# Tile loop of a graph layer: second one-hot half turned at the first tile, register loads behind queued work

## What is computed

```python
def head(w1, bb1, w2, bb2, a1, aab1, a2, aab2):
    feats = jnp.maximum(x @ w1 + bb1, 0.0) @ w2 + bb2
    x_cat = jnp.concatenate([feats[row], feats[col], elem[:, None]], axis=1)
    hid = jnp.maximum(x_cat @ a1 + aab1, 0.0)
    e1 = jax.nn.leaky_relu((hid @ a2 + aab2)[:, 0], negative_slope=0.2)
    w = jnp.exp(e1 - jnp.max(e1))
    pooled = jax.ops.segment_sum(w[:, None] * feats[col], row, num_segments=n)
    row_sum = jax.ops.segment_sum(w, row, num_segments=n) + 1e-10
    return pooled / row_sum[:, None]
...
x = _layernorm(x + gnn(x, edge_index, edge_weight), axis=-1)
```

## Time and profile before

| | |
|---|---|
| median of 3 runs | 5230.21 us (5229.04 to 5233.76) |
| profiled execution | 5190.44 us, span 5188.7 us |
| PE busy | 4402.2 us (85%) |
| DVE busy | 4550.7 us (88%) |
| ACT busy | 3761.1 us (72%) |
| POOL busy | 2702.7 us (52%) |
| mean granted PE clock | 0.956 |
| tile loop, mean DMA rate | about 218 GB/s |

### The profile page before, as it was taken

How to read it: one execution, slowest core, us unless ns; L and a number is a source line. 1 busy time by engine, 2 the same in 40 slices (tenths; PEclk the granted TensorE clock), 3 DMA queues, 4 the chain that set the end, 5 groups by cost and what they waited for, 6 DMA issues and landing times.

```text
span 5188.7 us, 133139 instructions
## 1 busy us (share of the span) xinstructions
PE 4402.2 (85%) x24914; PEld 3093.9 (60%) x24915; DVE 4550.7 (88%) x25629; ACT 3761.1 (72%) x12720; POOL 2702.7 (52%) x2834
## 2 busy tenths in 40 slices
PE   1499899999986899999999999999999999999920
PEld 0255555555554666767677767767677767767610
DVE  7799999999998789888899889889898889898853
ACT  0467766766762688888888888888888888888832
POOL 1266666666666555555555555555555555555522
PEclk9799999999997999999999999999999999999965
DMA  2032333333333777777777777777777777777623
GB/s 79 23 73 67 78 72 71 75 74 72 69 78 93 227 216 218 218 219 217 216 218 217 217 218 219 217 218 216 217 218 216 219 215 219 215 220 216 200 87 117
DMA packets 287022, 850.50 MB, mean 164 GB/s; under 512 B 98946, under 2 KB 138114, under 8 KB 286966
## 3 DMA queue, kind: packets, MB, share of 16 engines
q0 software_dynamic: 169920, 673.54, 46.8%
q1 hardware_dynamic: 74638, 160.14, 9.7%
q10 hardware_dynamic: 42408, 16.21, 1.2%
HBM read 738.46 MB, written 111.26 MB: 164 GB/s over the span
## 4 chain that ended last, share of the span: by engine, by line
PE 29%; ACT 25%; DVE 6%; issue 4%; DMA 4%; DVEq 1%; POOL 0%; ACTq 0%; POOLq 0%; SPq 0%
ACT z L1092 17%; PE psum L949 12%; PE psum L953 7%; PE psum L936 6%; DVE z L1503 3%; ACT onehot L1121 3%; DMA out_dram<-z 3%; ACT onehot_t L1110 3%; PE psum L962 2%; ACT onehot L1125 2%; PE psum L973 1%; DVE z L1493 1%; PE psum L921 1%; DVE acc L1552 1%; DVEq L1552 0%
## 5 line engine op out<-in xcount | busy, mean ns | idle before, releaser
L734 POOL DMA_INDIRECT z<-qf_table,rec x1664 | 1593.6, 958 | 1567.0 <-PE psum L936 1035.8
L1092 ACT ACTIVATE z<-z 128x64 f32<-128x64 f32 x6656 | 1651.5, 336 | 56.6 <-ACT z L1099 56.3
L949 PE MATMUL psum<-p_win,onehot_t 128*128 x9984 | 1434.0, 276 | 207.7 <-ACT onehot_t L1110 90.5
L949 PEld LDWEIGHTS psum<-p_win,onehot_t 128*128 128x128 bf16 x9984 | 963.9, 97 | 777.8 <-issue 460.6
L936 PE MATMUL psum<-z,onehot 128*128 128x260 f32 x3328 | 1027.2, 391 | 2.8 <-DVE acc L1552 1.9
L953 PE MATMUL psum<-z,ident 128*128 128x258 f32 x3328 | 1004.0, 383 | 0.0
L1503 DVE SCALAR_TENSOR_TENSOR z<-z,a_b 128x129 f32<-128x129 f32 x3328 | 893.0, 292 | 0.0
L1503 DVE SCALAR_TENSOR_TENSOR z<-psum,a_b 128x129 f32<-128x129 f32 x3328 | 822.6, 283 | 0.0
L1552 DVE TENSOR_TENSOR acc<-acc,psum 125x260 f32 x1664 | 698.7, 420 | 78.6 <-PE psum L936 48.8
L1493 DVE TENSOR_TENSOR z<-z,psum 128x258 f32<-128x258 f32 x1664 | 691.9, 416 | 39.4 <-PE psum L953 29.6
L666 POOL DMA_INDIRECT sorted_rows<-z x300 | 483.3, 1611 | 406.9 <-DVE z L1384 162.4
(11 more groups left out here) (221 smaller groups left out, 6363.0 us busy)
## 6 DMA issues: line engine op xcount, KB each, us to landing
p_table<-acc SPq DMA_DIRECT2D x100, 377.9 KB
p_win<-p_table SPq DMA_DIRECT2D x100, 377.9 KB
qf_table<-acc SPq DMA_DIRECT2D x75, 378.9 KB
z<-qf_table,rec POOLq DMA_INDIRECT x1664, 4.6
acc<-in_x_dram SPq DMA_DIRECT2D x25, 500.0 KB
z<-in_x_dram SPq DMA_DIRECT2D x20, 625.0 KB
out_dram<-z ACTq DMA_DIRECT2D x20, 625.0 KB
qf_table<-z SPq DMA_DIRECT2D x25, 378.9 KB
```

What stands on the lines that cost most here:

```text
L734: pool.indirect_dma_start(out=z_t[:, o + j, :], out_offset=None, in_=qf_table, in_offset=bass.IndirectOffsetOnAxis(ap=rec[:, o + j, 3:4].b ...
L949: mm = pe.matmul(to, onehot_t[:, j, :], p_flat[:, bass.ds((w % 2) * (3 * ZW) + (part * ZW + o), n)], start=(part == 0), stop=(part == 2 an ...
L1092: op = act.activation(z_t[:, slot, o:o + DO], z_t[:, slot, o:o + DO], ACT.Copy, scale=z_t[:, slot, o + DO:o + HF])
```

## The change

- PE turns half 1 of a step behind tile 0 instead of tile 2.
- ACT copies it between the weights of tiles 5 and 6 of its step before, not at the head of the step.
- PE does the sum of a step's last tile at the head of the step after, behind that step's first register load, and has one more step at its end for it.
- The register loads are taken apart: on PE one at the head of a step and one between the product and the sum of tile 3; on DVE one behind the adds of tile 0 and one behind those of tile 4.
- On DVE, the accumulator's scaling and the adds of the sums come behind the tile's own dot products instead of ahead of them.

```diff
--- before.py
+++ after.py
@@ -464,7 +464,7 @@
             return nc.s_assert_within((pack // (1 << 7 * j)) % 128 if j else pack % 128, 0, W - 1,
                                       skip_runtime_bounds_check_because="the table is clipped at W - 1")
 
-        def pipeline(eng, step):
+        def pipeline(eng, step, extra=0):
 
             step(-1, SPB - 1)
             for k in range(SPB):
@@ -472,7 +472,7 @@
             with nc.Fori(1, BODIES, engines=bass.OrderedEngineSet([eng.engine]), hint_back_edge=True) as i:
                 for k in range(SPB):
                     step(i, k)
-            for n in range(BODIES * SPB, NSB + 2):
+            for n in range(BODIES * SPB, NSB + 2 + extra):
                 step(n // SPB, n % SPB)
 
 
@@ -928,9 +928,13 @@
                 def tile(off, j):
                     return i * RING + (k + off) * SB + j
 
-                def sum_up(j):
-
-                    t, slot = tile(-2, j), ((k - 2) * SB + j) % RING
+                def load_windows(q):
+
+                    packs[q] = pe.value_load(win_pack[0:1, bass.ds((i * SPB + k) * (SB // 4) + q, 1)], min_val=0, max_val=(1 << 28) - 1)
+
+                def sum_up(off, j):
+
+                    t, slot = tile(off, j), ((k + off) * SB + j) % RING
                     pe.wait_ge(s_wf, t + 1)
                     since(pe, s_acc, t - 1)
                     pe.matmul(psum[:, 4 + j % 2, 0:H * HF], onehot[:, slot, :], z_t[:, slot, ZW:QW], start=True, stop=True)\
@@ -973,13 +977,15 @@
                     pe.matmul(psum[:, 7, P:P + H], ones_f[0:H, :], max_diag[:, (k - 1) % SPB, :], start=True, stop=True)\
                       .then_inc(s_max_b, 1)
 
+                packs = [None] * (SB // 4)
                 if live(i, k, 0):
-                    packs = [pe.value_load(win_pack[0:1, bass.ds((i * SPB + k) * (SB // 4) + q, 1)], min_val=0, max_val=(1 << 28) - 1)
-                             for q in range(SB // 4)]
+                    load_windows(0)
+                if live(i, k, -3):
+                    sum_up(-3, SB - 1)
                 for j in range(SB):
                     if live(i, k, 0):
                         hidden_src(j)
-                    if j == SB // 4 and live(i, k, 0):
+                    if j == 0 and live(i, k, 0):
                         turn(0, 1)
                     if j == SB // 4 and live(i, k, -1):
                         max_t()
@@ -987,10 +993,12 @@
                         max_to_all()
                     if j == SB - SB // 4 and live(i, k, 1):
                         turn(1, 0)
-                    if live(i, k, -2):
-                        sum_up(j)
-
-            pipeline(pe, step)
+                    if j % 4 == 3 and j < SB - 1 and live(i, k, 0):
+                        load_windows(j // 4 + 1)
+                    if j < SB - 1 and live(i, k, -2):
+                        sum_up(-2, j)
+
+            pipeline(pe, step, extra=1)
 
 
             pe.wait_ge(s_c_pick, KS)
@@ -1130,8 +1138,6 @@
                     act.dma_start(rec[:, kn * SB:(kn + 1) * SB, :].rearrange("p t n -> p (t n)"),
                                   rec_d[:, bass.ds((i * SPB + (k + 2)) * (SB * 4), SB * 4)]).then_inc(s_rec[kn], 16)
 
-                if live(i, k, 0):
-                    take_turned(0, 1)
                 if live(i, k, 1):
                     onehots(1, 0)
                 if live(i, k, -1):
@@ -1145,6 +1151,8 @@
                         take_turned(1, 0)
                     if j == SB // 2 and live(i, k, 1):
                         onehots(1, 1)
+                    if j == SB - 3 and live(i, k, 1):
+                        take_turned(1, 1)
 
             pipeline(act, step)
 
@@ -1478,9 +1486,11 @@
                 def sbn(off):
                     return i * SPB + (k + off)
 
-                if live(i, k, -2):
-                    packs = [dve.value_load(win_pack[0:1, bass.ds(sbn(-2) * (SB // 4) + q, 1)], min_val=0, max_val=(1 << 28) - 1)
-                             for q in range(SB // 4)]
+                packs = [None] * (SB // 4)
+
+                def load_windows(q):
+                    packs[q] = dve.value_load(win_pack[0:1, bass.ds(sbn(-2) * (SB // 4) + q, 1)], min_val=0, max_val=(1 << 28) - 1)
+
                 kk, kp, o = (k - 1) % SPB, (k - 2) % SPB, (k - 1) % SPB * SB
                 ev, er = e_val[:, o:o + SB, :], e_raw[:, o:o + SB, :]
 
@@ -1560,21 +1570,23 @@
                        .then_inc(s_decayed, 1)
 
                 Q = SB // 4
-                before_row = {0: [(-2, decay_sums)]}
                 chain = {0: [(-1, bias), (-1, leaky), (-1, tiles_max)], Q: [(-1, heads_max), (-1, diagonal)],
                          2 * Q: [(-1, new_shift), (-1, shifted)]}
                 for j in range(SB):
-                    for off, work, *args in before_row.get(j, []):
-                        if live(i, k, off):
-                            work(*args)
                     if live(i, k, 0):
                         add_rows(j)
-                    between = [(-2, add_sums, j)] + chain.get(j, [])
+                    if j % 4 == 0 and live(i, k, -2):
+                        load_windows(j // 4)
+                    between = chain.get(j, [])
                     for n in range(max(H - PEH, len(between))):
+                        if n < H - PEH and live(i, k, 0):
+                            own_dot(j, n)
                         if n < len(between) and live(i, k, between[n][0]):
                             between[n][1](*between[n][2:])
-                        if n < H - PEH and live(i, k, 0):
-                            own_dot(j, n)
+                    if live(i, k, -2):
+                        if j == 0:
+                            decay_sums()
+                        add_sums(j)
 
             pipeline(dve, step)
 
```

## The result

The changed kernel takes 6025.83 us (median of 4 runs, 6019.9 to 6026.52) against 5230.3 us for the kernel before: a ratio of 1.1517, interval 1.1497 to 1.1537. It is 796 us slower, 3.86 us for each of the 206 steps of the ring; the forecast was 750 us and 3.64 us.

What follows compares the result with a forecast made beforehand. A 15.58 us ring of waits between PE and ACT was taken as the bound. The new ring 17.5 + load 0.2 + clock 1.5 = 19.2 us, 3.64 above 15.56; 206 x 3.64 = 750, so 5230 + 750 = 5980 us, range 5600 to 6200.

Steps and rivals of the forecast that it cites:

- the ring: Tile 4's product on PE, ACT's first-half copy and second-half one-hots, PE's turn, back to that product: 17.5 us a step.
- step 2: PE's turn moved behind tile 0 waits for ACT's one-hots and closes a ring of 17.47, say 17.5 us a step.
- step 6: PE's clock falls after 2.6 to 3.0 us idle at the turn: 1.5 us a step, between 0 and 3.4.
- The mean of 2.0 us from the earlier trace: Full-speed work lost on PE after each of twenty idle stretches before the tile loop, in the profile before the change.
- step 3: Register loads: nothing gained on DVE; PE's load between tile 3's product and sum adds 0.2 us a step.
- The bound of 0.66: Upper limit in us for one PE register load, from two loads together; the range was 0 to 0.66.
- steps 4 and 5: Last tile's sum behind the next head on PE, decay and sum behind DVE's dot products: nothing, the latter -0.1 to +0.1.
- own range: Range for the main case, wait and clock fall: 5830 to 6200 us around 5980, chance 0.62.
- The old ring: Tile 4's product, first-half turn, ACT's copies of both halves and work between, back to that product: 15.58 us, the period.
- step 1: ACT's second-half copy ahead of weights six and seven cuts the 15.58 us ring: alone worth up to 1.7 us a step.
- That the clock stays: Rival: PE's turn waits but the idle stretch is too short to lower the clock: 17.7 us a step, 5671 us, chance 0.20.
- The faster side: Rival: ACT's one-hots are ready when PE reaches the turn, so PE's 13.9 us plus 0.4 decide: 4970 us, chance 0.08.

Runs made afterwards that it cites:

- the kernel with the filler: The changed kernel with 20 products of the identity with itself on PE behind tile 0, ahead of the waiting turn: 5595.46 us, ratio 1.0703.
- the first experiment: The changed kernel with only PE's turn of the second half put back behind tile 2: 5048.23 us, ratio 0.9657.
- the third experiment: The kernel before with only the turn behind tile 0 and the copy between weights 5 and 6: 6033.06 us, ratio 1.1546.
- the second experiment: The changed kernel with turn and copy put back, leaving only register loads, late eighth sum and DVE's order changed: 5217.52 us, ratio 0.9981.

## Why the prediction was right

**The ring, step 2.** Its four edges in the changed kernel, from the timeline: H4 3015.69 to copy 3021.08, 5.39 (5.50 forecast); copy to the end of the one-hots, 6.31 (6.32); to the turn at 3027.45, 0.06 (0.05); turn to H4 at full clock, in the kernel with the filler 3000.67 to 3006.32, 5.65 (5.60). The sum is 17.41 against 17.47. The 13 periods of the changed kernel that kept the clock are 17.41 or 17.42 us long, and the filler's mean is 17.46. That the one line decides is shown by the first and the third experiment, that it does so by a ring, and not by a single wait, by the places behind tile 1 and the one-hots behind weight 2.

**The clock, step 6.** The mechanism was right and the size too small: 1.5 us a step forecast, 2.09 measured. Two terms of it failed. The idle stretch was put at 2.6 to 3.0 us and is 3.0 to 3.9 in 194 of 199 steps, because H0 comes earlier than thought: it now starts 1.54 us behind H7 like any tile (3021.24 to 3022.78), where it took 2.40 (3007.13 to 3009.53 in the kernel before), and 0.3 to 0.6 us of that were counted. The load at the head costs PE nothing, L957 to S7 takes 3003.16 to 3003.61. And the mean of 2.0 us from the earlier trace rows was lowered to 1.5 for a shorter stretch and for loss inside the idle time; 2.0 would have been nearly right. The earlier trace rows had nothing, 1.7 or 3.4 us lost, in 4, 8 and 8 of 20; here it is nothing in 13 periods of 199, 1.5 us in the mean in 92 and 2.9 in 94. By the Trainium skill, "TensorE: Matmul & The Clock Gate", section "HAM oscillation — how this bites in real kernels", parted bursts of matmuls pay in every burst; the trace agrees nearly, with a fall in 186 periods of 199.

**The register loads, step 3.** On DVE at nothing: right, 10 us in all in the second experiment. On PE 0.2 us were put on the ring; the changed kernel shows 0 there. The bound of 0.66 was sound all the same: once the one-hots held PE up less, the same load cost up to 0.46 us, 0.21 in the mean. The changed kernel's trace has a load by itself (L933): 0.30 us. The Trainium skill's 0.2 us a register load ("Runtime: NRT & Kernel Launch", section "Instruction fetch mechanics"), by which it vanishes behind H3, is lower than that 0.30; that it vanishes agrees with the changed kernel (0) and not with the first experiment (up to 0.46 behind 1.1 us of queued products).

**The late sum and DVE's order, steps 4 and 5.** At nothing; together with the loads they gained 0.2% in the second experiment, and 0.3% that is not clear of noise by the third. Not foreseen was that ACT's first-half one-hots wait 665.3 / 153 = 4.3 us a step for the sum of tile 3, which stands behind the turn. It costs nothing, as ACT would wait for the exponentials anyway.

**The sum.** 17.47 + 0.2 + 1.5 = 19.2 forecast; 17.41 + 0 + 2.09 = 19.50 measured, the period in the trace. The clock's term was 0.6 us too small, the load's 0.2 too large, and that these erred in opposite ways, which brings the sum within 0.3 us, is luck. The difference was also worked out against 15.56 us from an execution of 5190 us and added to a median from a slower chip: between the two profiled executions it is 829 us, between the medians 796. And the own range of 5830 to 6200 us doesn't follow from its terms: 17.5 with 0 to 0.6 for the load and 0.7 to 2.6 for the clock is 18.2 to 20.7 us a step, 5774 to 6289 us. The old ring (step 1) was drawn as one path, though PE's 189.6 us of waiting were for the copy in 82.8 only and 64.5 for DVE. Breaking it helps all the same: the copy alone takes 2.5% off, 0.64 us a step ((5234.51 - 5103.45) / 206) of the 1.7 that were its upper end. The loads stand in the way of part of the rest.

**The rivals.** That the clock stays needed a filler to come true, at 5595 us for 5671 forecast. The faster side came true with the one-hots early or the turn behind tile 2, which is the condition named; the time, 4970, was met only once the one-hots and the second load had moved as well (4941 on a chip where the kernel before is 41 us faster, 4980 by the ratio).

## What to carry to other kernels

Before an instruction goes ahead in an in-order queue, follow its input back through every engine to the instruction itself one period earlier, and sum that ring with the work that now stands between; a ring can't be absorbed by engines sliding against each other, and it is longer by all that the instruction has overtaken. Two waits that each give nothing when removed alone may give something together, here 1.6 to 1.7%, if each is the other's slack. Where a new wait idles TensorE for some 3 us a period, price the clock with it; here that was more than half of the loss.

## What the hardware showed beside this

Twenty products of the identity, 2.35 us, kept the granted clock at 1.00 with 1.23 us still idle; so 128 x 128 products in f32 that only transpose did hold the clock up here. The falls by the idle stretch before the turn: none behind 149 stretches of up to 1.9 us and 11 behind 23 of 2.2 to 2.4 us (turn behind tile 1); in the changed kernel 1 behind 5 of 2.1 us, 61 behind 66 of 3.0 to 3.1, 120 behind 124 of 3.4 and 4 behind 4 of 3.9.

PE's signal of a turn's end came late on some chips and never on others. Normally ACT's waiting copy starts 0.39 us behind the start of the turn's last product. From 1800 to 4650 us, with the one-hots behind weight 1, on the second chip, it started more than 0.6 us behind in 177 of 183 copies that waited. The other kernels on that chip show it too, in a sixth to a third of such copies (32 of 182 behind tile 1), and those on the first in 3 to 9% (17 of 196 in the first experiment). On the third chip it shows in none of the 193 and 184 waiting copies of the two kernels that had them, and in none of 121 in the profile of the kernel before. That one kernel shows it in nearly every step goes with the place of its one-hots; the cause is open.

The chips differ otherwise too: the same kernel took 5189, 5227 and 5235 us on three of them.
